# Attention scores whose relative-position biases open the accumulation, one step ahead of the scores (fp32 transformer layer, one core)

## The chip, the cores and the metric

The kernel runs on one NeuronCore of a Trainium2 chip. The metric is the device time of one execution in microseconds (us), the median of several runs.

## The reference

The layer takes `x` of shape (2, 1024, 128) in fp32. It normalises each row, runs attention with 16 heads of 8 dimensions, adds the residual, normalises again, runs expert 0 of a small FFN (128 to 512 to 128, ReLU), normalises with gamma and beta, and adds the residual. The part that matters here is the attention:

```python
q, k, v = (x @ W.T + b, split in 16 heads of 8)
sim  = einsum('bhid,bhjd->bhij', q, k)
sim += transpose(rel_emb[bucket(i - j)], (2, 0, 1)) * SCALE   # 32 buckets; constant from a distance of under 128 on
sim += where(j > i, -inf, 0)
out  = softmax(sim) @ v ; out @ Wo.T + bo
```

The bucket of the far distances gives one constant a head, which cancels in the softmax. So only the "near" strip has a bias that must be added: from the diagonal (where the mask is) to a distance below 128.

## The kernel before, in words

Q and K are split into three bf16 parts each and stored to DRAM, so that a score is one bf16 matmul over 96 rows, plus 2 rows that carry minus the row maximum (`MROW`). The attention works on 8 groups of 4 heads (`G` = 8; 4 groups for each of 2 batches). `QA`, `KA` and the bias table `TT` are double buffered by group (index `p`).

A group has 12 steps, `STEPS`: for the query columns 0 to 511 (`ic` = 0) the key blocks `jb` 0 to 3, then for the columns 512 to 1023 (`ic` = 1) the key blocks 0 to 7. A step is 128 keys by `w` query columns, w = 512, 384, 256, 128 in steps 0 to 3, 512 in steps 4 to 8, then 384, 256, 128 in steps 9 to 11. For step s TensorE makes the scores of 4 heads in PSUM (`ST`, halves q = 0 and 1 of two heads, one bank a head), ScalarE takes the exp of one half at a time (`exps`, two activations a step) into `PT`, and TensorE multiplies by the values (`values`, into `OV`).

There is one set of score banks. So the scores of step s+1, half q, wait until the exp of step s, half q, has read the bank (semaphore `s_exp`). `exps` waits for `s_str`, which counts finished halves of scores.

Steps 0 to 3 and 7 to 11 have a near strip. There the bias is added in PSUM: for each head four matmuls of 32 output rows (the four column strips of the array, which run beside each other) multiply the constant matrix `flb` with a shifted window of `TT`. In the kernel before they come after both halves of the scores, and the last of them lets the exp begin.

Beside this the kernel finds the row maxima of the next group: 39 units (`UNITS`, 0 to 38), each one or a few score matmuls into one of three PSUM banks (`SM`, `NSM` = 3) and a VectorE maximum over it. A unit's matmul waits until VectorE has finished the unit three before it. `places()` spreads the units over the 12 steps and 3 positions of a step (0: after the scores of half 0; 1: after those of half 1; 2: at the end) in proportion to a cost that it estimates for each position. Units 13 and 38 are the transposes ("m") that turn the maxima into rows; their way is VectorE copy to `mrow`, then a DMA by SyncE (`move_m`) into `QA`, and the scores of step 0 (unit 13) or of step 4 (unit 38) of the group wait for it (`s_md`). Units 37 and 38 of a group lie in the group's own step 0, the others in the group before.

TensorE's order in step s (`group`) is: scores of s+1 half 0, units at 0, scores of s+1 half 1, units at 1, biases of s+1, values of s, units at 2. The last step works on step 0 of the next group. The last group has FFN tasks in place of units.

SyncE's queue is in order (`load`): for each group the mrow DMA of half 1, then the loads of the first half of `QA`/`KA` for the group after next, then, once `s_str` says that all 24 halves of the group's scores are done, the loads of the second half and of `TT` (6 DMAs), and behind them the next group's mrow DMA.

The program has loops: VectorE's and ScalarE's run over pairs of groups, TensorE's over groups 2 to 5.

Of the kernel before, what the change touches and what calls it, by code (L numbers as in the profile page):

```python
# [43 lines left out]
KST = MROW + 2  # L44
IC = 512
# [2 lines left out]
LSC = 2048.0  # L48
MASK16 = -60000.0
BW = 384  # L50
NEARU = 240


STEPS = [(ic, jb) for ic in range(N // IC) for jb in range(4 * (ic + 1))]
NSTEP = len(STEPS)
# [3 lines left out]
def step_cols(ic, jb):  # L59

    off = max(0, jb * 128 - ic * IC)
    return off, IC - off
# [28 lines left out]
assert NU % NSM == 0  # L91


NEAR0, NEAR1 = 176, 240

def near_cols(ic, jb):

    i0 = ic * IC + step_cols(ic, jb)[0]  # L100
    out = []
    for c, n in enumerate((NEAR0, NEAR1)):
        end = min(jb * 128 + n, (ic + 1) * IC)
        if end > i0:
            out.append((c, i0 - jb * 128 + 64 - 64 * c, end - i0))
    return out


def unit_cost(u):

    if u[0] == "m":
        return 200
    if u[0] == "far":
        return len(u[2]) * u[4] + 60
    return len(u[2]) * ((128 if u[1] == 0 else 256) + 75)


def places():

    pts, t = [], 0.0
    for s in range(NSTEP):
        ic, jb = STEPS[(s + 1) % NSTEP]
        half = 2 * step_cols(ic, jb)[1] + (640 if near_cols(ic, jb) else 0)
        for pos, cost in enumerate((half, half, 4.2 * step_cols(*STEPS[s])[1])):
            t += cost
            pts.append((t, s, pos))
    costs = [unit_cost(u) for u in UNITS]  # L130
    out, own, done = {}, {}, 0.0
    for u in range(NU):
        at = t * (S_START + (S_END - S_START) * done / sum(costs[:-1]))
        if u == NU - 1:
            at = t * M1_AT
        done += costs[u]
        s, pos = next((s, pos) for c, s, pos in pts if c > at % t)
        (own if at >= t else out).setdefault((s, pos), []).append(u)
    return out, own


S_START, S_END, M1_AT = 0.15, 1.03, 1.06
NEXT_UNITS, OWN_UNITS = places()


# [40 lines left out]
def tasks_at(s):  # L186
    if s not in WITHIN_AT:
        return range(0)
    later = [v for k, v in WITHIN_AT.items() if k > s]
    return range(WITHIN_AT[s], min(later) if later else len(WITHIN))  # L190
# [16 lines left out]
def build(nc, x, early, late, vectors, table, out):  # L207
    ctx = ExitStack()
    with ctx:
        def sb(name, shape, dt=F32):  # L210
            return ctx.enter_context(nc.sbuf_tensor(name, shape, dt))

        def sem(name):
            return ctx.enter_context(nc.semaphore(name))
# [6 lines left out]
        QA = sb("QA", [128, 2, 2, HG, IC], BF16)  # L221
        KA = sb("KA", [128, 2, 2, HG, IC], BF16)
        TT = sb("TT", [128, 2, HG, NEARU], FP16)
        NB = sb("NB", [128, 2, HG, 256], BF16)
# [11 lines left out]
        flb = sb("flb", [128, 64 + 128], BF16)  # L236
# [38 lines left out]
        ST = ps[:, 0:4, :].rearrange("p (b h) n -> p b h n", b=2)  # L275
# [34 lines left out]
        s_ldt = [sem(f"s_ldt{p}") for p in range(2)]  # L310
# [8 lines left out]
        s_str = sem("s_str")  # L319
        s_exp = sem("s_exp")  # L320
# [26 lines left out]
        def _(sp):  # L347
# [36 lines left out]
            def load_tt(hg, p):  # L384
                for part in range(2):
                    sp.dma_start(TT[64 * part:64 * part + 64, p, :, :],
                                 bass.AP(f16_d, hg * (HG * 2 * BW) + part * BW, [[1, 64], [2 * BW, HG], [1, NEARU]])
                                 ).then_inc(s_ldt[p], 16)
# [535 lines left out]
        def _(pe):  # L924
# [55 lines left out]
            def unit(g, p, k):  # L980
# [22 lines left out]
                                                KA[0:KS, p, j // IC, h, j % IC:j % IC + n], start=True, stop=True)  # L1003
                last.then_inc(s_smr, 1)

            def scores(g, p, s, q):

                ic, jb = STEPS[s]
                off, w = step_cols(ic, jb)
                near = near_cols(ic, jb)  # L1010
                if q == 0 and jb == 0:
                    pe.wait_ge(s_md[ic], 32 * g + 32)
                pe.wait_ge(s_exp, 2 * NSTEP * g + 2 * s + q + 1)
                for h in range(2 * q, 2 * q + 2):
                    last = nc.tensor.matmul(ST[:, q, h % 2, off:off + w],  # L1015
                                            KA[0:KST, p, jb // 4, h, (jb % 4) * 128:(jb % 4 + 1) * 128],
                                            QA[0:KST, p, ic, h, off:off + w], start=True, stop=not near,
                                            skip_group_check=True)
                if not near:
                    last.then_inc(s_str, 1)  # L1020

            def biases(p, s):

                ic, jb = STEPS[s]
                off, w = step_cols(ic, jb)
                near = near_cols(ic, jb)
                for q in range(2 if near else 0):
                    for h in range(2 * q, 2 * q + 2):
                        for c, u0, n in near:
                            for e in range(2):  # L1030
                                r0 = 64 * c + 32 * e
                                last = nc.tensor.matmul(ST[r0:r0 + 32, q, h % 2, off:off + n], flb[:, 32 * e:32 * e + 32],  # L1032
                                                        TT[:, p, h, u0:u0 + n], start=False, stop=True,
                                                        skip_group_check=True)
                    last.then_inc(s_str, 1)

            def values(g, p, s):
                ic, jb = STEPS[s]
                off, w = step_cols(ic, jb)
                if jb == 0:  # L1040
                    pe.wait_ge(s_ov, 2 * g + ic + 2)
                pe.wait_ge(s_exp, 2 * NSTEP * g + 2 * s + 4)
                for h in range(HG):
                    last = nc.tensor.matmul(OV[32 * h:32 * h + 2 * HD, off:off + w], VG[:, p, jb, h, :],  # L1044
                                            PT[:, s % 3, h, off:off + w], start=(jb == 0),
                                            stop=(jb == 4 * ic + 3), skip_group_check=True)
                last.then_inc(s_pv, 1)
# [48 lines left out]
            def group(g, p, load, last=False, first=False):  # L1096

                def s_units_at(s, pos):
                    for k in (OWN_UNITS0 if first else OWN_UNITS).get((s, pos), []):
                        unit(g, p, k)  # L1100
                    if not last:
                        for k in (NEXT_UNITS0 if first else NEXT_UNITS).get((s, pos), []):
                            if k in HALF_UNITS:
                                pe.wait_ge(s_ldqk[1 - p][HALF_UNITS[k]], 64 * load)
                            unit(g + 1, 1 - p, k)

                for s in range(NSTEP):
                    if s + 1 < NSTEP:
                        at = (g, p, s + 1)
                    else:  # L1110
                        at = None if last else (g + 1, 1 - p, 0)
                        if not last:
                            pe.wait_ge(s_ldt[1 - p], 32 * load)
                    if at:
                        scores(*at, 0)
                    s_units_at(s, 0)
                    if at:
                        scores(*at, 1)
                    s_units_at(s, 1)
                    if at:  # L1120
                        biases(*at[1:])
                    if s == 0:
                        pe.wait_ge(s_vg, g + 1)
                    values(g, p, s)
                    s_units_at(s, 2)
                    if last:
                        for n in tasks_at(s):
                            task(n)
# [23 lines left out]
            nc.tensor.matmul(ps[0:64, 0, 0:64], flb[:, 0:64], flb[:, 0:64], start=True, stop=True).then_inc(s_pv, 3)  # L1152
            pe.wait_ge(s_ldt[0], 32)
            for q in range(2):
                scores(0, 0, 0, q)
                unit(0, 0, OWN0 + q)
            biases(0, 0)
            group(0, 0, 1, first=True)
            group(1, 1, 2)
            with pe.Fori(1, G // 2 - 1) as r:  # L1160
                for p in range(2):
                    group(2 * r + p, p, r + 1 + p)
# [101 lines left out]
```

## Time and profile before

| | us |
|---|---|
| median of 3 runs | 406.53 (405.81 to 408.67) |
| the profiled execution | 405.76 |
| its span on the core | 403.9 |
| TensorE busy | 321.9 (80%) |
| VectorE busy | 288.2 (71%) |
| ScalarE busy | 183.9 (46%) |
| scores of step 4, groups 0 to 7, begin at | 99.15, 137.99, 173.38, 207.60, 242.07, 276.18, 310.23, 343.15 |

The profile is of one execution; the span leaves out some 2 us around it. Busy times overlap between engines. The last line is the beat of the kernel: one group takes some 34 us, and the eight groups take the stretch from 79 us to 365 us of the span. Its first number is of the group whose start still has a slow TensorE clock.

### The profile page before, as it was taken

The numbers are of one execution on the slowest core, as the hardware profiler recorded it, in microseconds if no ns is written. First come the engines' busy times: TensorE is split into PE (matmuls) and PEld (weight loads), VectorE is DVE, ScalarE is ACT, GpSimd is POOL, SyncE is SP. The second block draws the span as 40 slices with busy tenths as digits, with TensorE's granted clock in tenths as the row PEclk, the third lists the DMA queues.
The fourth block names the chain that finished last, engine by engine and source line by source line (L and its number), as shares of the span: only waits on it lengthen the run. The fifth ranks groups of instructions, "written<-read, shape, count | busy, mean of one in ns | idle before, by whom it ended". The sixth has DMA issues, their size and how long they took to land.

```text
span 403.9 us, 9250 instructions
## 1 busy us (share of the span) xinstructions
PE 321.9 (80%) x3197; PEld 152.9 (38%) x3197; DVE 288.2 (71%) x960; ACT 183.9 (46%) x258; POOL 69.6 (17%) x78
## 2 busy tenths in 40 slices
PE   0282438396999799889989979988998998999982
PEld 0131215143234334434433433443444344346752
DVE  3985356358668478588868848867885996773986
ACT  1042024132555455565555456556455555774330
POOL 9812035700001000100100010010010000161552
PEclk9996586668699899999999999999999999999997
DMA  8013422410011201201110121222123010200011
GB/s 234 17 52 116 144 88 94 147 64 3 3 45 42 60 2 61 84 4 46 60 42 17 49 87 23 76 78 41 38 71 88 15 18 9 33 2 11 4 54 52
DMA packets 18297, 21.95 MB, mean 54 GB/s; under 512 B 5584, under 2 KB 14960, under 8 KB 18256
## 3 DMA queue, kind: packets, MB, share of 16 engines
q1 hardware_dynamic: 18256, 21.45, 18.2%
q8 instruction: 20, 0.33, 0.3%
q14 instruction: 21, 0.17, 0.1%
HBM read 14.98 MB, written 4.23 MB: 48 GB/s over the span
## 4 chain that ended last, share of the span: by engine, by line
PE 47%; DVE 18%; DMA 14%; issue 8%; ACT 5%; SPq 4%; POOL 1%; DVEq 0%; ACTq 0%; POOLq 0%
PE ps L1015 13%; PE ps L1001 12%; PE ps L1044 12%; DMA QA<-mrow 6%; ACT PT L626 5%; PE ps L1032 5%; DMA qk_scratch<-QS 4%; DVE FM L759 4%; DVE junk L766 3%; DVE XN L701 2%; DMA KA<-qk_scratch 2%; DMA rows<-in_vectors 2%; PE ps L1077 2%; DVE st L836 1%; SPq L394 1%
## 5 line engine op out<-in xcount | busy, mean ns | idle before, releaser
L626 ACT ACTIVATE PT<-ps 128x1024 f32<-128x1024 f32 (+1 forms) x192 | 145.8, 810 | 135.4 <-PE ps L1032 106.7
L759 DVE TENSOR_REDUCE FM<-ps 128x1 f32<-128x512 f32 (+3 forms) x176 | 108.5, 660 | 30.3 <-PE ps L1001 29.6
L1001 PE MATMUL ps<-KA,QA 96*128 96x256 bf16 (+3 forms) x544 | 108.7, 293 | 18.4 <-DMA KA<-qk_scratch 14.5
L1015 PE MATMUL ps<-QA,KA 98*128 98x512 bf16 (+3 forms) x384 | 98.1, 341 | 26.1 <-DMA QA<-mrow 9.8
L766 DVE CUSTOM_DVE_ANT_0 junk<-ps,NB 128x256 bf16<-128x256 f32 (+1 forms) x224 | 79.0, 403 | 32.0 <-PE ps L1001 31.7
L1044 PE MATMUL ps<-PT,VG 128*16 128x512 f32 (+3 forms) x768 | 86.6, 497 | 0.0
L1001 PEld LDWEIGHTS ps<-KA,QA 96*128 96x128 bf16 x544 | 44.2, 101 | 105.3 <-DVE FM L759 31.1
L1015 PEld LDWEIGHTS ps<-QA,KA 98*128 98x128 bf16 x384 | 31.8, 100 | 53.8 <-ACT PT L626 25.2
L497 POOL COPY NB<-NBH 128x1024 bf16 (+1 forms) x7 | 7.3, 1041 | 216.7 <-PE ps L1044 215.8
L1032 PE MATMUL ps<-TT,flb 128*32 128x176 f16 (+4 forms) x1152 | 38.9, 245 | 0.0
L1032 PEld LDWEIGHTS ps<-TT,flb 128*32 128x32 bf16 x1152 | 21.5, 96 | 17.7 <-issue 16.9
L1044 PEld LDWEIGHTS ps<-PT,VG 128*16 128x16 f32 x768 | 21.2, 97 | 9.6 <-issue 8.2
L766 DVE DVE_READ_ACCUMULATOR2_ANT FM<- 128x1 f32 x256 | 21.2, 83 | 1.1 <-issue 1.1
L766 DVE CUSTOM_DVE_ANT_0 junk<-ps,NBH 128x256 bf16<-128x256 f32 (+1 forms) x32 | 11.2, 403 | 10.7 <-PE ps L1001 10.5
L932 PE MATMUL ps<-early_s,XN 128*128 128x128 f32 x16 | 4.1, 425 | 18.1 <-DVE XN L701 18.1
L1077 PE MATMUL ps<-QS,late_s 128*128 128x512 f32 x32 | 15.8, 611 | 0.8 <-ACT QS L653 0.8
L754 DVE COPY mrow<-ps 8x512 bf16<-8x512 bf16 x16 | 6.5, 408 | 12.1 <-PE ps L1001 6.5
L545 POOL TENSOR_SCALAR tmp<-mv 128x4 f32<-128x4 f32 x8 | 2.3, 286 | 69.7 <-DVE mv L839 69.7
L585 ACT ACTIVATE QS<-ps,early_s 128x512 bf16<-128x512 f32 x8 | 5.5, 688 | 17.1 <-PE ps L938 17.1
L701 DVE TENSOR_SCALAR XN<-X,mv,rs 128x128 f32<-128x128 f32 x16 | 11.5, 1284 | 0.1
L938 PE MATMUL ps<-xnT,early_s 128*128 128x512 f32 x16 | 11.0, 800 | 0.0
L932 PEld LDWEIGHTS ps<-early_s,XN 128*128 128x128 f32 x16 | 3.2, 224 | 18.9 <-issue 16.4
(88 smaller groups left out, 255.6 us busy)
## 6 DMA issues: line engine op xcount, KB each, us to landing
QA<-qk_scratch SPq DMA_DIRECT2D x48, 96.0 KB
KA<-qk_scratch SPq DMA_DIRECT2D x16, 288.0 KB
TT<-f_scratch SPq DMA_DIRECT2D x16, 120.0 KB, 7.0
qk_scratch<-QS SPq DMA_DIRECT2D x4, 384.0 KB
qk_scratch<-QS SPq DMA_DIRECT2D x12, 128.0 KB
X<-in_x SPq DMA_DIRECT2D x2, 512.0 KB, 6.2
out<-U SPq DMA_DIRECT2D x4, 256.0 KB, 2.3
xnT<-OT SPq DMA_DIRECT2D x28, 32.0 KB
```

Of the source, the lines that this page charges most:

```text
L497: nc.gpsimd.tensor_copy(NB[:, p, :, :], NBH[:, bass.ds(HG * hg, HG), :]).then_inc(s_nb, 1)
L626: nc.scalar.activation(PT[:, s % 3, 2 * q:2 * q + 2, off:off + w], ST[:, q, :, off:off + w], ACT.Exp).then_inc(s_exp, 1)
L701: last = nc.vector.tensor_scalar(XN[:, t, :], X[:, t, :], mv[:, t, 0:1], rs[:, t:t + 1], ALU.subtract, ALU.mult)
L759: nc.vector.tensor_reduce(FM[:, ib, heads[0]:heads[-1] + 1, piece], bank[:, 0:w * len(heads)].rearrange("p (h n) -> p h n", n=w), AX.X, AL ...
L766: last = nc.vector.tensor_tensor_reduce(junk[:, k % NSM, i, 0:w], bank[:, i * w:(i + 1) * w], nb[:, h, 256 - w:256], 1.0, NEG, ALU.add, AL ...
L932: last = nc.tensor.transpose(ps[:, BANK["T", b, half], i * 128:(i + 1) * 128], XN[:, b * TPB + 4 * half + i, :], idf[:, :])
L938: nc.tensor.matmul(ps[:, BANK["QK"[qk], b, c], :], (wq_s, wk_s)[qk][:, :], xnT[:, b, c * IC:(c + 1) * IC], start=True, stop=True).then_inc ...
L1001: last = nc.tensor.matmul(bank[:, i * w + j - j0:i * w + j - j0 + n], QA[0:KS, p, ib // 4, h, (ib % 4) * 128:(ib % 4 + 1) * 128], KA[0:KS, ...
L1015: last = nc.tensor.matmul(ST[:, q, h % 2, off:off + w], KA[0:KST, p, jb // 4, h, (jb % 4) * 128:(jb % 4 + 1) * 128], QA[0:KST, p, ic, h, o ...
L1032: last = nc.tensor.matmul(ST[r0:r0 + 32, q, h % 2, off:off + n], flb[:, 32 * e:32 * e + 32], TT[:, p, h, u0:u0 + n], start=False, stop=Tru ...
L1044: last = nc.tensor.matmul(OV[32 * h:32 * h + 2 * HD, off:off + w], VG[:, p, jb, h, :], PT[:, s % 3, h, off:off + w], start=(jb == 0), stop ...
L1077: last = nc.tensor.matmul(bank, w1_s[:, f * 128:(f + 1) * 128], tT[:, c % 2, :], start=True, stop=True)
```

## The change

Three things change. The bias matmuls of a step are now the first of the accumulation (`start=True`, 240 columns in all four strips, where two strips had 176; 128 columns where the step has no more, 112 in step 7), and they are issued a step ahead: at the end of step s, behind the values, come the biases of step s+2, whose half q waits for the exp of step s+1, half q. The scores of a near step are two matmuls a head: one adds onto the biased columns, one begins fresh on the columns behind them (272 columns in steps 0 and 8, 144 in 1 and 9, 16 in 2 and 10, 400 in 7; none in 3 and 11). Each half of the scores now lets its exp begin by itself. `places()` counts other costs (no bias in the first two positions, 1200 or 450 more in the third), so that units move: unit 3 from the end of step 2 to position 0 of step 3, unit 7 to the end of step 4, unit 14 from step 6 to the end of step 5, others between. `TT` has 304 columns instead of 240, so its DMA rows are 608 bytes instead of 480. The wait for `TT` of the next group stands a step earlier.

```diff
-NEARU = 240
+NEARU = 304
...
-NEAR0, NEAR1 = 176, 240
+NEAR = 240
...
     i0 = ic * IC + step_cols(ic, jb)[0]
-    out = []
-    for c, n in enumerate((NEAR0, NEAR1)):
-        end = min(jb * 128 + n, (ic + 1) * IC)
-        if end > i0:
-            out.append((c, i0 - jb * 128 + 64 - 64 * c, end - i0))
-    return out
+    return max(0, min(jb * 128 + NEAR, (ic + 1) * IC) - i0)
...
-        half = 2 * step_cols(ic, jb)[1] + (640 if near_cols(ic, jb) else 0)
-        for pos, cost in enumerate((half, half, 4.2 * step_cols(*STEPS[s])[1])):
+        half = 2 * step_cols(ic, jb)[1]
+        ahead = 1200 if near_cols(*STEPS[(s + 2) % NSTEP]) else 450
+        for pos, cost in enumerate((half, half, 4.2 * step_cols(*STEPS[s])[1] + ahead)):
...
+            def biases(g, p, s, q):
...
+                pe.wait_ge(s_exp, 2 * NSTEP * g + 2 * s + q + 1)
+                for h in range(2 * q, 2 * q + 2):
+                    for e in range(4):
+                        c, r0 = e // 2, 32 * (e % 2)
+                        nc.tensor.matmul(ST[32 * e:32 * e + 32, q, h % 2, off:off + near], flb[:, r0:r0 + 32],
+                                         TT[:, p, h, u0 - 64 * c:u0 - 64 * c + near], start=True, stop=False,
+                                         skip_group_check=True)
...
-                pe.wait_ge(s_exp, 2 * NSTEP * g + 2 * s + q + 1)
+                if not near:
+                    pe.wait_ge(s_exp, 2 * NSTEP * g + 2 * s + q + 1)
                 for h in range(2 * q, 2 * q + 2):
-                    last = nc.tensor.matmul(ST[:, q, h % 2, off:off + w],
...
-                if not near:
-                    last.then_inc(s_str, 1)
...
+                    for a, b, fresh in ((off, off + near, False), (off + near, off + w, True)):
+                        if b > a:
+                            last = nc.tensor.matmul(ST[:, q, h % 2, a:b],
+                                                    KA[0:KST, p, jb // 4, h, (jb % 4) * 128:(jb % 4 + 1) * 128],
+                                                    QA[0:KST, p, ic, h, a:b], start=fresh, stop=True,
+                                                    skip_group_check=True)
+                last.then_inc(s_str, 1)
...
                 for s in range(NSTEP):
...
                     s_units_at(s, 1)
-                    if at:
-                        biases(*at[1:])
                     if s == 0:
                         pe.wait_ge(s_vg, g + 1)
                     values(g, p, s)
+                    if ahead:
+                        if s + 2 == NSTEP:
+                            pe.wait_ge(s_ldt[1 - p], 32 * load)
+                        for q in range(2):
+                            biases(*ahead, q)
                     s_units_at(s, 2)
```

## Rows read from the trace of the kernel before

**Rows 1.** The page: engines' busy time and instructions, then the costliest groups of instructions.

```profile
PE 321.9 (80%) x3197; PEld 152.9 (38%) x3197; DVE 288.2 (71%) x960; ACT 183.9 (46%) x258; POOL 69.6 (17%) x78
...
L626 ACT ACTIVATE PT<-ps 128x1024 f32<-128x1024 f32 (+1 forms) x192 | 145.8, 810 | 135.4 <-PE ps L1032 106.7
...
L759 DVE TENSOR_REDUCE FM<-ps 128x1 f32<-128x512 f32 (+3 forms) x176 | 108.5, 660 | 30.3 <-PE ps L1001 29.6
...
L1015 PEld LDWEIGHTS ps<-QA,KA 98*128 98x128 bf16 x384 | 31.8, 100 | 53.8 <-ACT PT L626 25.2
...
L1032 PE MATMUL ps<-TT,flb 128*32 128x176 f16 (+4 forms) x1152 | 38.9, 245 | 0.0
```

**Rows 2.** Busy time by engine: steps 6 to 10, 3 to 5, 11 to 3.

```profile
215.70:229.90 14.20, 14.20 (x175) 6.36 (x174) 12.60 (x40) 7.01 (x10) 0.00 (x0) 1.00 0.13 45
207.60:215.70 8.10, 7.72 (x55) 2.73 (x55) 5.85 (x24) 6.20 (x7) 0.00 (x0) 1.00 0.00 0
229.90:242.00 12.10, 9.36 (x137) 4.72 (x135) 7.03 (x33) 5.79 (x10) 1.39 (x2) 1.00 0.23 73
```

**Rows 3.** Timeline of TensorE: start, length, instructions, idle time before them, releaser.

```profile
207.60 0.60 PE L1015 MATMUL ps<-QA,KA 98*128 98x512 bf16 x2 [1.60 <-DMA QA<-mrow]
...
212.28 0.60 PE L1015 MATMUL ps<-QA,KA 98*128 98x512 bf16 x2
...
215.71 0.61 PE L1015 MATMUL ps<-QA,KA 98*128 98x512 bf16 x2
...
216.98 0.39 PE L1001 MATMUL ps<-KA,QA 96*128 96x128 bf16 x4
...
220.68 0.49 PE L1032 MATMUL ps<-TT,flb 128*32 128x176 f16 x14
...
221.11 1.03 PE L1044 MATMUL ps<-PT,VG 128*16 128x512 f32 x6
...
228.18 0.28 PE L1015 MATMUL ps<-QA,KA 98*128 98x128 bf16 x2
...
229.94 0.60 PE L1015 MATMUL ps<-QA,KA 98*128 98x512 bf16 x2
...
233.15 0.50 PE L1015 MATMUL ps<-QA,KA 98*128 98x384 bf16 x2 [0.79 <-ACT PT L626]
...
242.07 0.60 PE L1015 MATMUL ps<-QA,KA 98*128 98x512 bf16 x2 [1.40 <-DMA QA<-mrow]
```

**Rows 4.** Timeline of the SyncE queue: DMA issues.

```profile
195.51 2.60 SPq L379 DMA_DIRECT2D QA<-qk_scratch  x3
...
202.43 15.35 SPq L394 DMA_DIRECT2D QA<-mrow  x4
...
229.59 2.54 SPq L379 DMA_DIRECT2D QA<-qk_scratch  x3
```

**Rows 5.** Timeline of ScalarE, same stretch.

```profile
212.92 1.94 ACT L626 ACTIVATE PT<-ps 128x1024 f32<-128x1024 f32 x2 [0.34 <-PE ps L1015]
...
227.29 1.09 ACT L626 ACTIVATE PT<-ps 128x512 f32<-128x512 f32 x2 [1.44 <-PE ps L1032]
```

**Rows 6.** Timeline of VectorE, same stretch.

```profile
208.57 0.42 DVE L766 CUSTOM_DVE_ANT_0 junk<-ps,NB 128x256 bf16<-128x256 f32 x1 [1.28 <-PE ps L1001]
...
214.71 1.49 DVE L759 TENSOR_REDUCE FM<-ps 128x1 f32<-128x384 f32 x3
...
234.83 0.20 DVE L777 TENSOR_REDUCE NM<-FM 128x16 f32<-128x48 f32 x1
```

**Rows 7.** Chain of waits in order of time (start, length, what).

```profile
232.07 1.03 ACT PT L626
...
235.42 3.10 issue
...
238.71 0.42 DVE mrow L754
...
239.90 2.06 DMA QA<-mrow
```

More of the change, by code:

```diff
@@ L1004, in unit @@
                 last.then_inc(s_smr, 1)
+            def biases(g, p, s, q):
+                ic, jb = STEPS[s]
+                off, w = step_cols(ic, jb)
+                near = near_cols(ic, jb)
+                if not near:
+                    return
+                u0 = ic * IC + off - jb * 128 + 64
+                pe.wait_ge(s_exp, 2 * NSTEP * g + 2 * s + q + 1)
[5 more added lines that the diff above has]
+                                         skip_group_check=True)
             def scores(g, p, s, q):
@@ L1012, in scores @@
                     pe.wait_ge(s_md[ic], 32 * g + 32)
-                pe.wait_ge(s_exp, 2 * NSTEP * g + 2 * s + q + 1)
+                if not near:
+                    pe.wait_ge(s_exp, 2 * NSTEP * g + 2 * s + q + 1)
                 for h in range(2 * q, 2 * q + 2):
-                    last = nc.tensor.matmul(ST[:, q, h % 2, off:off + w],
-                                            KA[0:KST, p, jb // 4, h, (jb % 4) * 128:(jb % 4 + 1) * 128],
-                                            QA[0:KST, p, ic, h, off:off + w], start=True, stop=not near,
-                                            skip_group_check=True)
-                if not near:
-                    last.then_inc(s_str, 1)
[L1022 to L1035, printed above, removed]
+                    for a, b, fresh in ((off, off + near, False), (off + near, off + w, True)):
[5 more added lines that the diff above has]
+                last.then_inc(s_str, 1)
             def values(g, p, s):
@@ L1107, in group @@
                 for s in range(NSTEP):
[L1108 to L1113, printed above, removed]
+                    at, ahead = ((g, p, s + k) if s + k < NSTEP else
+                                 None if last else (g + 1, 1 - p, s + k - NSTEP) for k in (1, 2))
                     if at:
@@ L1154, in _ @@
             for q in range(2):
+                biases(0, 0, 0, q)
+            for q in range(2):
                 scores(0, 0, 0, q)
                 unit(0, 0, OWN0 + q)
-            biases(0, 0)
+            for q in range(2):
+                biases(0, 0, 1, q)
             group(0, 0, 1, first=True)
```

## Prediction

> **What bounds the kernel now.** I read the page first [rows 1]. TensorE is busy 80% of the span. ScalarE waited 106.7 us on the bias matmuls (L1032), which the change is aimed at; but ScalarE is busy only 46%, and its idle time costs something only where another engine then waits for it. So the second view is the busy time by stretch of one group [rows 2]. Steps 6 to 10 are TensorE alone: 14.20 us busy of 14.20, with VectorE at 12.60. In steps 3 to 5 TensorE has 0.38 us of idle time. The idle time is in the change of groups (9.36 busy of 12.10).
>
> The third view is the timeline of TensorE [rows 3], which gives the gaps: 0.79 us at 233.15, where scores wait for an exp, and 1.40 us at 242.07 (1.60 us at 207.60), where the scores of step 4 wait for the mrow DMA.
>
> The fourth view, the SyncE queue [rows 4], says what sets that last wait. The loads at the end of a group's scores start at 195.51, and the scores of step 4 begin at 207.60, 12.1 us later; in the next group 229.59 and 242.07, 12.5 us. The same distance in the four other groups that load is 12.2 to 12.4 us. The mrow DMA is behind these loads in the queue. Issued at 202.43 it ends its wait only some 5 us later, while one issued when they have drained takes 2.06 us [rows 7]. So in most groups the beat is: scores of step 4, then some 22 us to the last `s_str` of the group (207.60 to 229.59), then 12.3 us of loads. What happens in steps 11 and 0 to 3 is hidden behind the loads.
>
> There is a second way to the same point: unit 37, the maxima (234.83 [rows 6]), unit 38, the copy to mrow, the DMA. From the maxima to step 4 this takes 242.07 - 234.83 = 7.2 us where VectorE's loop turns back; 3.10 us of that are "issue" time before the copy [rows 7]. Without them it is some 4.1 us. So this way ends last only in the two groups with a turn of the loop (2 and 4); in the others it would allow step 4 some 2 us earlier than the loads do.
>
> **The bias work itself.** It stays as large. The four strips of a head run beside each other: 16 matmuls occupy 220.68 to 221.11, 0.43 us for four heads, which is 4 x 240 columns at the full clock (granted 1.00 in rows 2, 2.4 GHz). So the two strips that grow from 176 to 240 columns cost nothing; their cover is the two that already had 240. One set leaves the path between scores and exp and stands again behind the values, 0.
>
> **The split scores.** 28 more matmuls a group (7 steps x 4 heads), 224 in all, each with its own weight load (equal counts in rows 1). Columns are the same. Four matmuls of 128 columns with four weight loads take 216.98 to 217.30, with the turn to the bias matmuls in it, so at most 80 ns each and, taking 0.1 us off for that turn, 55 ns: a load is hidden from 128 columns on. The pieces of 16 columns stand alone: 7 ns of columns against a load of some 54 ns, 47 ns each, 4 in step 9 of each group (0.19 us) and 4 in step 1, behind the loads. Lower bound for all pieces: 0.05 us a group; a gain is excluded, as work is only added. Upper bound: each load costs its 100 ns [rows 1], 2.8 us a group. I take 0.2 us between step 3 and the last `s_str`, as in the row of 128 columns the loads are hidden. The Trainium skill ("TensorE: Matmul & The Clock Gate", part 3, The mechanism) says that a weight load overlaps matmuls in flight only when the row group differs. By that rule all 224 loads would show, and the sum would be the upper bound; the row of 55 ns speaks against it, since these loads have the same row group.
>
> **The new wait.** The biases of step s+2, half 1, wait for the exp of step s+1, half 1, and behind them on TensorE are queued the units of position 2, all of the next step, and thereby ScalarE and VectorE. Count from t, the start of the scores of s+1. Exp begins at t + 0.64 (212.28 to 212.92 [rows 3, 5]) and both halves take 1.94, so with 0.05 for the semaphore the wait is over at t + 2.63 at 512 columns. TensorE arrives at 0.43 + units + 0.43 + units + 0.1 (turn) + values 0.86 (the 1.03 at 221.11 less the 0.17 by which a matmul's end trails its columns) + 0.1 + first bias half 0.1 to 0.2. That is 2.41 in step 5 (units 0.38), so 0.22 us of new stall; 2.56 in steps 6 and 7 (units 0.43), 0.07 each; step 8 none (the exps are shorter, 1.51). In step 9 scores of 0.22 twice and values of 0.65 arrive at 1.38 against 0.42 + 1.09 + 0.05 = 1.55, 0.17. Step 10 and step 0 none. Step 11: arrival 1.92 against 2.63, 0.71 us. The last takes the place of the 0.79 us before 233.15 (and of 0.2 us at the half after it): the exps begin 1.5 us earlier there, but now TensorE waits for both halves where it waited for one, before unit 36, the next scores and unit 37.
>
> **The units.** They are the hidden part. Before, unit 3 was done while step 4 waited for the DMA (VectorE idles 1.28 us up to 208.57 [rows 6]); now it is issued after that wait, one reduce (mean 0.66 us [rows 1]) more for VectorE in the part that counts. Before step 5's scores at 212.28 there is one unit more on TensorE, 0.22 us. In step 5 the end position has units 11, 12, 13 and 14. Unit 13 needs the reduce of unit 10, unit 14 that of unit 11. The three reduces of 384 columns begin at 214.71 now and take 0.5 us each; with VectorE 0.6 us later, the second ends near 216.35. Unit 14 stands now ahead of step 6's scores, which began at 215.71, and would hold them to 216.56: 0.85 us later, of which 0.2 is unit 7, 0.22 the new stall, the rest unit 14. To steps 6 to 10 come 0.07 + 0.07 + 0.17 + 0.2 (split), less small changes of order: step 11 begins 231.1 instead of 229.94, +1.1 to 1.2.
>
> **The sum by groups.** The last `s_str` comes earlier in step 10 than it did: it waits neither for biases nor for two units, 0.4 us after the step's start instead of some 1.2. Step 10 starts 1.1 later (228.18 to 229.3), so the loads start at 229.85 instead of 229.59: +0.3 in groups 1, 3, 5 and 6, 4 x 0.3 = 1.2 us, and the rest of the delay is hidden by the loads. Cover gone, it would be 1.1 each. In groups 2 and 4 the maxima come at 235.95 instead of 234.83, 2 x 1.1 = 2.2 us. Group 0 (slow clock, units elsewhere, first biases ahead of the first scores) +0.3. The last group has TensorE full of FFN tasks and no units: the exps start earlier, the new waits and the tasks take it back, -1 to +0.5; with the reciprocals that load VectorE in group 6, I take +0.3. Sum 4.0 us. Against the profiled execution, 405.76 becomes 409.8; the median of 406.53 lies 0.77 higher, so 410.5.
>
> The DMA of `TT` grows from 120 to 152 KB a half. The Trainium skill ("DMA: Bandwidth & Descriptors", its table of limits) puts 512 bytes as the least transfer at full rate, with read-modify-write below. The rows go from 480 to 608 bytes, so by that rule the load would get cheaper instead of dearer. No row here separates its price from the 12.3 us, so the sum has 0, and the range takes 0.3 us a group either way.
>
> **Rivals.** (1) Faster: ScalarE's head start is what counts. The waits of 0.79 and 0.20 us at the change of groups vanish, no unit holds the scores of step 6, and the distance of 12.3 us is the chain of the maxima and not the loads: 7 changes of groups x 0.99 = 6.9, 399.6. For it speaks the large idle time of ScalarE; against it that 12.1 to 12.5 us recurs in six groups with different DMA waits, and the 0.71 that I count in step 11. It decides once TensorE reaches the bias half after the exp has ended.
> (2) No difference: the loads pin the beat and VectorE is not late at unit 14. Then the new stalls of steps 5 to 9 (0.5) are about paid by the shorter way to `s_str` (0.8): 0 to +1.5 us, 406.5 to 408. Against it is VectorE's 12.60 of 14.20.
> (3) Slower by more: the loads do not hide the change of groups, because mrow then ends last everywhere: 7 x 1.1 = 7.7, 414.2. It decides when the delay of the maxima passes 2 us in the unlooped groups.
> (4) The weight loads show: 16 of the 28 a group lie between step 3 and the last `s_str`, 8 x 16 x 0.1 = 12.8 us, 419.3 alone.
> (5) The change does not do what it says: the bias waits so long that exps begin no earlier. Then idle time before the exps stays above 100 us; it ends like (3).
>
> **Chances.** Forecast 0.38 (408.5 to 412.5), (1) 0.13, (2) 0.28, (3) with (5) 0.14, (4) 0.07. The predicted time is the forecast's, 410.5. The range reaches down over (2) and the near part of (1), up over (3): 403 to 416; outside lie some 0.1 below and 0.1 above. 1% (402.5 to 410.6) is about what a measurement of this kernel tells from no change: faster 0.12; the same 0.45, which is (2) and nearly half of the forecast; slower 0.43.
>
> **What would show it.** Bias matmuls with idle time before them, released by ScalarE, mostly in step 11 (0.7) and step 5 (0.2). The 12.3 us from the first load of a run to step 4 kept in groups 1, 3, 5 and 6. Step 6 of a group some 8.9 us after its step 4's scores instead of 8.1. ScalarE's idle time well under 135 us. Weight loads of the 128-column kind 608 instead of 384, with a mean near 100 ns, and TensorE's busy time in steps 6 to 10 grown by under 0.5 us. Wrong would be the prediction if the 12.3 us shrink (then faster), or if the pieces stretch steps 7 to 10 by more than a microsecond.

## The result and the profile after

The changed kernel takes 427.12 us (424.66 to 428.44, 4 runs) against 407.6 of the kernel before beside it (405.81 to 410.97, 4 runs): 1.046 times as long, 95% interval 1.038 to 1.055. The ratios, here and below, leave out executions that took over 1.5% longer than the fastest of their kernel; the medians leave out none. I had predicted 410.5 and 403 to 416. It is slower, as forecast, but by 19 us and not by 4.

The page of the profiled execution (428.44 us, span 426.6), the lines that answer to [rows 1], and one more:

```profile
PE 339.5 (80%) x3421; PEld 172.2 (40%) x3421; DVE 288.3 (68%) x960; ACT 184.5 (43%) x258; POOL 69.4 (16%) x78
...
q8 instruction: 30, 0.49, 0.5%
...
L622 ACT ACTIVATE PT<-ps 128x1024 f32<-128x1024 f32 (+1 forms) x192 | 146.4, 809 | 154.1 <-PE ps L1030 153.9
...
L755 DVE TENSOR_REDUCE FM<-ps 128x1 f32<-128x512 f32 (+3 forms) x176 | 109.0, 660 | 45.8 <-PE ps L997 45.1
...
L1030 PEld LDWEIGHTS ps<-QA,KA 98*128 98x128 bf16 x608 | 52.1, 101 | 47.4 <-issue 17.9
...
L1014 PE MATMUL ps<-TT,flb 128*32 128x240 f16 (+2 forms) x1152 | 47.6, 258 | 7.7 <-ACT PT L622 5.4
```

The 224 extra matmuls and loads are there, with the same 101 ns a load. ScalarE waits more than before (154 us against 135), not less: nothing became faster. The line q8 is the queue that brings TensorE's instructions, in packets of 16 KB (over all the runs below its count changes only with TensorE's program). The page of the kernel before has 20 of them:

```profile
q8 instruction: 20, 0.33, 0.3%
```

The exps do begin sooner behind their own scores. In step 9, at full clock, it is 0.61 us (270.88 to 271.49) where the kernel before has 1.83 us (222.51 to 224.34):

```profile
270.88 0.49 PE L1030 MATMUL ps<-QA,KA 98*128 98x240 bf16 x4
271.49 1.51 ACT L622 ACTIVATE PT<-ps 128x768 f32<-128x768 f32 x2 [1.43 <-PE ps L1030]
```
```profile
222.51 0.49 PE L1015 MATMUL ps<-QA,KA 98*128 98x384 bf16 x2
224.34 1.51 ACT L626 ACTIVATE PT<-ps 128x768 f32<-128x768 f32 x2 [1.21 <-PE ps L1032]
```

But the scores themselves come later by as much: counted from the scores of step 4 (254.75 and 207.60), this exp begins after 16.74 us in both kernels. TensorE is the full engine here, and moving work within it moved the exps nowhere.

Where the time went is told by the starts of step 4's scores, the beat of the kernel. They were 137.99, 173.38, 207.60, 242.07, 276.18 and 310.23 for groups 1 to 6, and are 138.10, 173.73, 210.18, 254.75, 290.26 and 327.10. Group 4's start alone falls back by 10 us. The timeline of TensorE there and in what follows, to be held against [rows 3]:

```profile
238.11 0.39 PE L1014 MATMUL ps<-TT,flb 128*32 128x240 f16 x8 [0.53 <-ACT PT L622]
238.43 0.39 PE L997 MATMUL ps<-KA,QA 96*128 96x256 bf16 x2
243.05 0.48 PE L1030 MATMUL ps<-QA,KA 98*128 98x240 bf16 x2 [4.23 <-issue]
246.34 0.48 PE L1030 MATMUL ps<-QA,KA 98*128 98x240 bf16 x2 [2.80 <-issue]
...
254.75 0.60 PE L1030 MATMUL ps<-QA,KA 98*128 98x512 bf16 x2 [0.88 <-DMA QA<-mrow]
...
263.72 0.60 PE L1030 MATMUL ps<-QA,KA 98*128 98x112 bf16 x4
...
290.26 0.83 PE L1030 MATMUL ps<-QA,KA 98*128 98x512 bf16 x2 [1.88 <-DMA QA<-mrow]
...
291.30 1.06 PE L1030 MATMUL ps<-QA,KA 98*128 98x512 bf16 x2
```

Three things are to be seen. At 238.82, where TensorE's loop over groups turns from group 3 to 4, it stands still for 4.23 us and, two matmuls later, for 2.80 us, and waits for nothing that the profile shows ("issue"). The granted clock falls during the first stop, so the price of the turn is more than the two gaps; the stretch behind it (the column after the engines is the granted clock, 0.50 is 1.2 GHz):

```profile
242.80:249.40 6.60, 3.54 (x18) 1.55 (x22) 1.33 (x7) 1.62 (x2) 0.00 (x0) 0.50 0.09 31
```

Behind 290.26 a pair of score matmuls takes 1.06 us where it takes 0.60 elsewhere: the clock. And the SyncE queue of that group, beside [rows 4], has a longer way from the first load to step 4: 290.26 - 277.16 = 13.1 us, before 12.3.

```profile
277.16 2.28 SPq L375 DMA_DIRECT2D QA<-qk_scratch  x3
...
285.38 1.37 SPq L390 DMA_DIRECT2D QA<-mrow  x2
```

The busy time of 10 us from step 4 on, in group 5 and in group 4:

```profile
290.20:300.20 10.00, 9.70 (x75) 3.95 (x75) 6.49 (x25) 6.40 (x7) 0.00 (x0) 0.83 0.11 16
255.00:265.00 10.00, 9.60 (x92) 4.30 (x90) 8.12 (x30) 6.76 (x8) 0.00 (x0) 1.00 0.17 25
```

TensorE gets 75 matmuls done where it gets 92 done at full clock. A mean of 0.83 is some 3.4 us at the lower level of 1.2 GHz. It falls after the wait for the mrow DMA, here 1.88 us. The same happens after 173.73 and 210.18, and for twice as long after 327.10, but not after 138.10, where the wait was 1.89 us. From group 1 on, the profiled execution of the kernel before has it only in group 1, after its one wait of 2.38 us.

### The profile page after: what moved, and what is told of

Its sections match the earlier page's. It is cut to its first block, busy times and chain, and to the rows that moved or that the text cites. A ratio compares the mean times of both kernels' runs of the same rounds, so it can differ in the third digit from the quotient of the medians.

```text
span 426.6 us, 9700 instructions
## 1 busy us (share of the span) xinstructions
PE 339.5 (80%) x3421; PEld 172.2 (40%) x3421; DVE 288.3 (68%) x960; ACT 184.5 (43%) x258; POOL 69.4 (16%) x78
## 3 DMA queue, kind: packets, MB, share of 16 engines
HBM read 15.51 MB, written 4.23 MB: 46 GB/s over the span
## 4 chain that ended last, share of the span: by engine, by line
PE 48%; DMA 15%; DVE 14%; issue 10%; ACT 8%; SPq 4%; POOL 1%; ACTq 0%; DVEq 0%; POOLq 0%
PE ps L997 13%; PE ps L1030 13%; PE ps L1043 11%; ACT PT L622 8%; DMA QA<-mrow 7%; PE ps L1014 6%; DMA qk_scratch<-QS 4%; DVE FM L755 3%; DVE XN L697 2%; DMA KA<-qk_scratch 2%; DMA rows<-in_vectors 2%; PE ps L1076 1%; DVE st L832 1%; DVE junk L762 1%; DVE U L885 1%
## 5 line engine op out<-in xcount | busy, mean ns | idle before, releaser
L1030 PE MATMUL ps<-QA,KA 98*128 98x240 bf16 (+3 forms) x608 | 98.9, 283 | 24.6 <-DMA QA<-mrow 16.6
L1043 PE MATMUL ps<-PT,VG 128*16 128x512 f32 (+3 forms) x768 | 85.1, 517 | 0.0
L1030 PEld LDWEIGHTS ps<-QA,KA 98*128 98x128 bf16 x608 | 52.1, 101 | 47.4 <-issue 17.9
L1014 PE MATMUL ps<-TT,flb 128*32 128x240 f16 (+2 forms) x1152 | 47.6, 258 | 7.7 <-ACT PT L622 5.4
L1014 PEld LDWEIGHTS ps<-TT,flb 128*32 128x32 bf16 x1152 | 24.6, 97 | 58.0 <-ACT PT L622 42.4
L1043 PEld LDWEIGHTS ps<-PT,VG 128*16 128x16 f32 x768 | 12.7, 96 | 23.0 <-issue 17.0
L841 DVE TENSOR_TENSOR QS<-ps,X 128x512 f32<-128x512 f32 x4 | 2.7, 683 | 12.4 <-PE ps L1067 12.4
```

What stands on the lines that cost most here:

```text
L1014: nc.tensor.matmul(ST[32 * e:32 * e + 32, q, h % 2, off:off + near], flb[:, r0:r0 + 32], TT[:, p, h, u0 - 64 * c:u0 - 64 * c + near], star ...
L1030: last = nc.tensor.matmul(ST[:, q, h % 2, a:b], KA[0:KST, p, jb // 4, h, (jb % 4) * 128:(jb % 4 + 1) * 128], QA[0:KST, p, ic, h, a:b], sta ...
```

## The experiments

The runs of the kernel before spread more than I had thought (405 to 421 us), and the longer ones have the lower clock: the mean granted clock is 0.925 in the one of 405.93 us and 0.890 in the one of 421.03 us. In its profiled execution the waits of 1.4 to 1.6 us before step 4 bring no fall to half clock; b_unroll below, the same kernel but for a loop written out, has four falls in its own. So ratios are given, each against runs of the kernel before beside it on the same chip; of the kernel called b_tt, whose executions spread most, only the range.

**The turn of the loop.** Written out instead of looped, in the changed kernel and in the kernel before:

```diff
-            with pe.Fori(1, G // 2 - 1) as r:
+            for r in range(1, G // 2 - 1):
```

> The changed kernel with TensorE's loop over groups 2 to 5 written out, so that it has no turn; nothing else differs. Theory (instruction fetch: the loop body has outgrown the instruction buffer, and the 4.23 and 2.80 us of idle time behind the turn are its refetch): both gaps vanish, with them the half clock behind them; 8 to 10 us faster than the changed kernel, 417 to 419, some 2.5% above the kernel before. Rival (the gaps are waits of the new order, which merely fall there): they stay, 425 to 428.

Measured (a_unroll): 420.14 us, ratio 1.029 (1.021 to 1.037). Both gaps are gone; the scores behind the bias matmuls of the group change follow at once. That is 7.0 us of the 19.5, a little less than the 8 to 10 expected.

> The kernel before with the same loop written out. Theory: its loop body fits, the turn costs nothing that shows (scores at 233.15 start 0.05 us after the exp that they wait for), so no difference within 1%. Rival (straight code is better or worse for every version, by another way): the same step of 8 to 10 us would appear here, or a loss by more instruction fetching.

Measured (b_unroll): 409.47 us, ratio 0.997 (0.991 to 1.003). In the kernel before the turn costs nothing that can be told from zero. So the loop as such is not the cause. (The profiled execution, 414.15 us, has falls to half clock after its waits of 2.09, 1.75, 1.62 and 1.63 us before step 4: the spread again.) Is it the new order, or the length of the body? The kernel before with split scores, in its old order:

```diff
-                    last = nc.tensor.matmul(ST[:, q, h % 2, off:off + w],
...
+                    cut = off + max([n for _, _, n in near], default=0)
+                    for a, b in ((off, cut), (cut, off + w)):
+                        if b > a:
+                            last = nc.tensor.matmul(ST[:, q, h % 2, a:b],
```

> The kernel before with the scores of near steps in two matmuls a head, in the old order, the biases behind them, units as before: 224 more matmuls and weight loads, and a loop body as long as the changed kernel's. Theory (size of the loop body): a gap of some 7 us behind the turn of TensorE's loop at about 232 us, as in the changed kernel, plus under 0.3 us a group for the pieces: 414 to 417. Rival A (the gap comes from the new order, not from size): no gap, 407 to 409. Rival B (weight loads show, 0.1 us each): 16 to 28 x 0.1 us a group, steps 7 to 10 stretched, 418 or more, with or without the gap.

The output of this kernel leaves the near scores out; it serves for its times alone. Measured (b_split): 416.78 us, ratio 1.020 (1.012 to 1.028). The gaps are there, in the old order, and the instruction queue has its 30 packets:

```profile
239.87 0.50 PE L1018 MATMUL ps<-QA,KA 98*128 98x240 bf16 x4 [3.00 <-issue]
...
243.37 0.59 PE L1035 MATMUL ps<-TT,flb 128*32 128x240 f16 x8 [2.13 <-issue]
```
```profile
q8 instruction: 30, 0.49, 0.5%
```

And the other way round, the new order with a short body:

```diff
-                    for a, b, fresh in ((off, off + near, False), (off + near, off + w, True)):
+                    for a, b, fresh in ((off, off + w, True),):
...
-                                         ST[:, q, :, off:off + w], ACT.Exp).then_inc(s_exp, 1)
+                                         ST[:, q, :, off:off + w], ACT.Exp, scale=1e-3).then_inc(s_exp, 1)
```

> The changed kernel with one fresh matmul a head for the scores (the bias underneath is overwritten, so the output leaves the biases and the mask out; the exp is taken of a thousandth of the score, to keep it finite). TensorE's loop body loses 56 matmuls and 56 weight loads. Theory (size): the gaps behind the turn vanish as in the written-out version, 416 to 419. Rival A (order): gaps stay, 424 to 427. Rival B (weight loads): both the gaps stay and steps 7 to 10 get 0.4 us shorter each.

Measured (a_one): 419.21 us, ratio 1.025 (1.017 to 1.033), no gaps, 20 instruction packets. So the length of the loop body decides, not the order. Of the body, the extra pieces are 28 matmuls and 28 weight loads a group, two groups long. With the short body the queue brings its 20 packets and none comes during the loop's second round (none between 227.5 and 305.4 us in the kernel before, none between 231.4 and 315.2 in a_one); with the long one there are 10 more, 8 of them between 240.2 and 304.4 in the change. And the stops end with them: in the change a packet starts at 240.26 and one at 243.55, and TensorE goes on 2.79 us behind each; in b_split it is 2.58 and 2.51 us (packets at 237.29 and 240.86). Written out, the changed kernel has 27 packets and no stop, so fetching straight on is hidden, and what shows is the fetch after the jump back. That the body no longer fits into what the sequencer keeps is the reading that fits all four runs; the buffer itself no trace shows.

**The width of TT.** The wider table alone, in the kernel before:

```diff
-NEARU = 240
+NEARU = 304
```

> The kernel before with TT 304 columns wide (DMA rows of 608 bytes), nothing else. Theory (the load ahead of the mrow DMA got longer with the wider table): the distance from the first load to the scores of step 4 goes from 12.0 to 12.5 us to 12.6 to 13.2, which is 0.7 x 5 = 3 to 4 us, and the waits before step 4 pass 1.9 us and bring the half clock more often: 411 to 416. Rival (the distance grew because of the new order): unchanged distances and time, within 1%.

Measured (b_tt): 414.78 to 426.68 us in four runs (median 422.78, above the 411 to 416 expected), with the kernel before at 405.95 to 416.38 beside it. The profiled execution is the longest of the four. From the first load to step 4 it is now 12.6 to 13.3 us in all six groups. SyncE's queue, TensorE's step 4 and the 10 us behind one of them:

```profile
202.94 2.60 SPq L379 DMA_DIRECT2D QA<-qk_scratch  x3
...
209.87 1.39 SPq L394 DMA_DIRECT2D QA<-mrow  x2
```
```profile
215.54 1.03 PE L1015 MATMUL ps<-QA,KA 98*128 98x512 bf16 x2 [2.10 <-DMA QA<-mrow]
```
```profile
178.00:188.00 10.00, 10.00 (x50) 3.34 (x51) 5.45 (x23) 6.44 (x7) 0.00 (x0) 0.66 0.00 0
```

The mrow DMA is issued 6.9 us after the first load, as before, but lands later, TensorE waits 1.7 to 3.3 us instead of mostly 1.2 to 1.6, and in this execution each of the six waits is followed by some 6.8 us at 1.2 GHz (0.66 of the clock over 10 us, 50 matmuls for 88). From the scores of step 4 to the last `s_str` it is then 24.5 to 25.0 us, for 21.8 to 22.1 at full clock. In the changed kernel the wide load can be taken back, since columns 240 and on hold zeros:

```diff
+            nc.gpsimd.memset(TT[:, :, :, LOADU:NEARU], 0.0).then_inc(s_zero, 1)
...
-                                 bass.AP(f16_d, hg * (HG * 2 * BW) + part * BW, [[1, 64], [2 * BW, HG], [1, NEARU]])
+                                 bass.AP(f16_d, hg * (HG * 2 * BW) + part * BW, [[1, 64], [2 * BW, HG], [1, LOADU]])
```

> The changed kernel, loops and placement as in the change, but only 240 columns of TT are loaded (rows of 480 bytes, as before); columns 240 to 303 hold no bias and are set to zero once. Theory (three causes: turn of the loop 7 us, wider TT with the half clock behind it, placement of units): the distance from load to step 4 goes back from 12.4 to 13.2 to 12.0 to 12.5 us, 3 to 8 us faster than the changed kernel, 418 to 424, the gaps at the turn stay. Rival (the wide load matters only in the old order): 425 to 428.

Measured (a_zero): 420.52 us, ratio 1.032 (1.023 to 1.042): 6.6 us less than the change. The distances are 12.0 to 12.3 us again (13.3 in group 2, where VectorE's loop turns, and 20.2 in group 4, where both loops turn). The gaps at the turn of TensorE's loop stay, 3.86 and 2.76 us, and end 2.58 and 2.71 us behind a packet of its instruction queue.

**The placement of the units.** The changed kernel, loop written out, with the old costs in `places()`:

```diff
-        half = 2 * step_cols(ic, jb)[1]
-        ahead = 1200 if near_cols(*STEPS[(s + 2) % NSTEP]) else 450
-        for pos, cost in enumerate((half, half, 4.2 * step_cols(*STEPS[s])[1] + ahead)):
+        half = 2 * step_cols(ic, jb)[1] + (640 if near_cols(ic, jb) else 0)
+        for pos, cost in enumerate((half, half, 4.2 * step_cols(*STEPS[s])[1])):
```

> The changed kernel, loop written out, and units placed by the old costs. Theory (unit 14 ahead of step 6's scores and unit 3 behind step 4's wait make each group 0.5 to 0.9 us longer from step 4 to the last s_str): 22.4 goes to 21.8, 2 to 4 us faster than the written-out version, 415 to 418. Rival (placement doesn't matter, the waits for exps do): 419 to 421.

Measured (a_unroll_units): 415.35 us, ratio 1.012 (1.006 to 1.018), 4.8 us less than with the new placement. The timeline of group 2:

```profile
170.73 0.61 PE L1029 MATMUL ps<-QA,KA 98*128 98x512 bf16 x2 [1.29 <-DMA QA<-mrow]
...
179.00 0.61 PE L1029 MATMUL ps<-QA,KA 98*128 98x112 bf16 x4
```

The scores with which TensorE opens its step 6 (they are those of step 7, hence the pieces of 112 columns) begin 8.27 us after the scores of step 4, with unit 14 behind them; in the change it is 263.72 - 254.75 = 8.97. From the scores of step 4 to the last `s_str` it is 21.6 to 21.9 us in groups at full clock, where the change has 22.4 to 22.6 and the kernel before 21.8 to 22.1.

**What pins the beat.** If the loads ahead of mrow do, it should help to put the two TT loads of a group behind the next mrow DMA:

```diff
                 move_m(p, 1, g)
+                if g:
+                    load_tt((g + 1) % GPB, 1 - p)
...
                 load_half(g + 2, p, 1)
-                load_tt(hg, p)
...
-            with sp.Fori(0, G // 2 - 2) as r:
+            for r in range(G // 2 - 2):
```

> The kernel before with the two TT loads of a group issued behind the next mrow DMA instead of before it, and SyncE's loop written out for that. Theory (the beat is 12.3 us of loads ahead of the mrow DMA, and TT is part of them): the mrow DMA is issued at the same time but lands 1 to 3 us earlier in five groups; the wait before step 4 falls under 1 us and the half clock behind it vanishes: 398 to 403. Rival (the other loads, of QA and KA, are the backlog, or the wait has another source): 405 to 408.

Measured (b_late): 397.7 us (396.41 to 399.78), ratio 0.971 (0.962 to 0.980), a faster kernel than both. SyncE's queue and TensorE's step 4 in group 3:

```profile
191.96 2.12 SPq L379 DMA_DIRECT2D QA<-qk_scratch  x3
...
199.17 1.28 SPq L394 DMA_DIRECT2D QA<-mrow  x2
200.49 1.37 SPq L386 DMA_DIRECT2D TT<-f_scratch  x2
```
```profile
203.22 0.60 PE L1017 MATMUL ps<-QA,KA 98*128 98x512 bf16 x2 [0.43 <-DMA QA<-mrow]
```

The mrow DMA, issued 7.2 us after the first load (6.9 before), now has its scores running 4.05 us later instead of 5.2 (202.43 to 207.60 in [rows 4] and [rows 3]). The wait is 0.43 us instead of 1.60, and no stretch at 1.2 GHz follows any step 4, not even behind the wait of 2.37 us in group 2. The distance from the first load to step 4 is 10.7 to 11.3 us in four of the six groups, where it was 12.1 to 12.4; in groups 2 and 4, where VectorE's loop turns, it is 13.35 and 11.9. SyncE's loop is written out here too, but the way gets shorter in groups 1, 3, 5 and 6 alike and not only at its turn. The same in the changed kernel, loop written out:

> The changed kernel, TensorE's loop written out, with the two TT loads behind the next mrow DMA. Theory (wider loads ahead of mrow, and the half clock that follows the long wait, make up most of what is left): distances 12.6 to 13.2 fall under 12, no half clock behind step 4: 403 to 410, 10 us or more faster than the written-out version. Rival (the rest is the new order's own): above 415.

Measured (a_late): 408.74 us, ratio 1.001 (0.996 to 1.005): 11.4 us faster than the written-out version. Its longest wait is now in group 2, 3.39 us, where VectorE's loop turns ahead of the copy to mrow; a fall to half clock of 3.4 us follows it, the only one behind a step 4 from group 1 on.

**What the new order is worth by itself.** All side effects out: loop written out, 240 loaded columns, old placement, TT behind mrow.

> The change with its three side effects taken out: TensorE's loop written out, 240 loaded columns, units by the old costs, and the TT loads behind the mrow DMA. What is left is the new order and the split scores. Theory (new order costs 0.5 us of waits for exps a group and gives nothing): 398 to 402, 1 to 4 us behind the same version of the kernel before (397.7). Rival (once the rest is gone, exps that start earlier win): 390 to 396.

Measured (a_best): 402.48 us, ratio 0.988 (0.983 to 0.994), just above the 398 to 402 expected. With one score matmul a head on top (as in a_one):

> As the one above, but one fresh score matmul a head (leaves out biases and mask, exp of a thousandth of the score). Theory (a hidden weight load a piece, 47 ns only for the pieces of 16 columns): 1 to 2 us faster than it. Rival (weight loads show, 28 x 0.1 us a group): over 10 us faster.

Measured (a_best_one): 400.62 us, ratio 0.985 (0.979 to 0.991). That is 1.9 us less, but not all of it is the price of the 224 pieces. In groups at full clock the two kernels are alike: 21.54 to 21.55 us from the scores of step 4 to the last `s_str` in both, and 32.27 and 32.23 us from step 4 to step 4 (groups 5 to 6). So the pieces cost under 0.1 us a group, and the rest of the 1.9 us goes with the longer falls to half clock at the turns of VectorE's loop (10.2 and 3.4 us in the profiled execution of a_best, 6.8 us in this one). The kernel before with the same DMA order is at 397.7, so some 5 us were still open. They might be the order, or the turn of VectorE's loop, which comes in two groups:

```diff
-            with dve.Fori(0, G // 2 - 1) as r:
+            for r in range(G // 2 - 1):
```

> The kernel before with TT loaded behind the mrow DMA, and VectorE's loop over pairs of groups written out too. Theory (with the loads gone from the way of mrow, its turn of 3.1 us before the copy to mrow ends last in groups 2 and 4, where step 4 still waited 2.37 and 1.00 us): 393 to 396. Rival (fetching straight code costs as much): 397 to 400.

Measured (b_late_dve): 392.9 us, ratio 0.964 (0.958 to 0.970). The two turns cost 4.8 us once the loads were out of the way (by the ratios 0.7%, some 3 us, but the times of the two kernels do not overlap: b_late took at least 396.41 us, this one at most 393.8). Then the decisive pair, both without any turn of VectorE's loop:

> The change with its side effects taken out (TensorE's loop written out, 240 loaded columns, units by the old costs, TT behind the mrow DMA) and VectorE's loop written out as well. It differs from the run beside it in the new order and the split scores alone. Theory A (the 5 us by which the new order trailed came from the turns of VectorE's loop, whose 3.1 us land on a longer way and bring the half clock; elsewhere a group takes 32.3 us in both): 391 to 394, within 1% of the other. Theory B (the waits for exps and the pieces cost 0.6 us a group everywhere): 396 to 399.

> The kernel before with TT behind the mrow DMA and VectorE's loop written out, again, for a comparison on one chip. Both theories: 391 to 394.

Measured: 392.92 us (a_best_dve), ratio 0.961 (0.955 to 0.967), and 392.72 us (b_best), ratio 0.959 (0.953 to 0.966). No difference. So the same two turns of VectorE's loop cost the new order 9.6 us (402.48 to 392.92), twice what they cost the old one: as long as that loop stays, the new order is 4.8 us behind (402.48 against 397.7), and falls to half clock follow its waits at these turns, where b_late has none. The SyncE queue of the new order, first loads of groups 3 and 4:

```profile
185.53 2.12 SPq L375 DMA_DIRECT2D QA<-qk_scratch  x3
...
217.58 2.12 SPq L375 DMA_DIRECT2D QA<-qk_scratch  x3
```

and its busy time between them, then that of the old order over its group:

```profile
185.50:217.60 32.10, 31.29 (x394) 16.04 (x392) 25.84 (x95) 19.06 (x27) 1.38 (x2) 1.00 0.13 46
```
```profile
191.10:223.40 32.30, 30.90 (x368) 13.83 (x364) 25.89 (x95) 18.96 (x27) 1.38 (x2) 1.00 0.14 46
```

A group takes 32.05 us in the one and 32.3 in the other, at full clock in both. The new order has no gap at the change of groups (the old one keeps its 0.79 us before the scores of step 1), and TensorE is busy 0.4 us longer a group. That the gained gap pays for the waits for exps and the pieces is my reading; the runs show the sum.

## Why the prediction was wrong

The direction was that of the forecast (though I gave "the same within 1%" 0.45 and "slower" only 0.43), and much of the mechanism held; the size was out by a factor of almost five. Two terms that I had at nothing, the turn of TensorE's loop and the wider TT, are 13.6 of the 16.6 us by which the measured 427.1 lies above my 410.5. The differences, each from two kernels that differ in one thing:

| | counted | measured |
|---|---|---|
| turn of TensorE's loop | not named | 7.0 us (427.1 to 420.1) |
| wider TT | 0, bound 0.3 us a group | 6.6 us (427.1 to 420.5) |
| placement of the units | most of the 4 us | 4.8 us (420.1 to 415.4) |
| new order and pieces, VectorE's loop written out | waits 0.5, pieces 0.2 us a group | none in sum (392.9 and 392.7) |
| the same, VectorE's loop kept | the same | 4.8 us (402.5 and 397.7) |

Not all of them ran on one chip. By the ratios to the kernel before beside them, the first three are 7.2, 5.6 and 6.9 us and the last is 7.1 us, so each is good to some two microseconds; and each carries its share of falls to half clock, so they need not add up.

**The loop: the step that failed.** Under "The split scores" I priced 28 matmuls a group by their columns and weight loads and found them hidden. That was right where I looked: under 0.1 us a group at full clock, against the 0.2 counted. But instructions also have to be brought to the engine: at the turn TensorE stood still for 4.23 and 2.80 us, and its clock was at half for 6.8 us from 242.7 on. The kernel before turned its loop without a gap, so no row of it showed this price, and I took the price of a longer body for zero without saying so. b_split shows it in the old order, a_one shows the new order without it.

**TT: a term wrongly at zero.** I wrote that no row separates its price from the 12.3 us, and put 0. Yet I had just argued that everything ahead of the mrow DMA in the queue is in the beat. By my own argument 64 KB more per group had to count. It is some 0.7 us a group (12.6 to 13.3 us in b_tt), and the rest comes behind it: with the wait before step 4 near 2 us the clock falls in most groups, which adds 1.3 us (23.7 for 22.4, once to half clock for 3.4 us) to 2.8 us (24.8 for 22.0, in b_tt) to the group. The Trainium skill ("DMA: Bandwidth & Descriptors", Specifications) gives 512 bytes as the least transfer at full rate; by that the load should have become cheaper, as its rows grew from 480 to 608 bytes. Here it brings 27% more bytes too, and the way behind it is longer, so any gain from the row length is smaller than what the bytes cost; the runs decide.

**The clock.** I read granted 1.00 in the rows of one execution and took it as given. The same rows show the waits of 1.40 and 1.60 us, and in the same trace the one of 2.38 us in group 1 was followed by a fall. That was the warning. The clock also goes with the spread of the kernel before, from 405 to 421 us.

**The beat: right for the kernel before, too short for the change.** That loads of 12.3 us pin step 4 was confirmed by b_late, which takes TT out of them and gains 10 us or more. But the 12.3 us that I said would be kept in groups 1, 3, 5 and 6 became 12.8, 12.4, 13.1 and 13.2. With b_late rival (3) and the reverse of it, rival (1), fall: the distance was not the chain of the maxima. Rival (1) also expected ScalarE's head start to pay. I too had named idle time of ScalarE well under 135 us as a sign of being right; it is 154 us. That is also the sign of rival (5), above 100 us, but exps do begin sooner behind their scores (0.61 us for 1.83), so its reason, that the bias waits hold them up, falls. Rival (2) needed VectorE not to be late at unit 14, and it is late. Rival (4), weight loads that show, falls by a_best_one (at most 1.9 us for 224 pieces; 0.1 us each would be 22). I had set the rule of the Trainium skill ("TensorE: Matmul & The Clock Gate", part 3, The mechanism) on row groups aside for the row of 55 ns, and the run agrees.

**The waits for exps and the units: right in size.** The scores that open TensorE's step 6 were foretold 8.9 us after the scores of step 4 and come 8.97 us after; unit 14 is issued at 263.54, directly before them. From the scores of step 4 to the last `s_str` at full clock, 22.25 us follow from the prediction's numbers, and it is 22.4 to 22.6. In step 11 the second bias half waits: the first eight bias matmuls run at 237.19, the others at 238.11, 0.7 us of lost time as counted. What I did not expect is that these waits cost nothing in the end in the pair without side effects and without turns of VectorE's loop.

## What to carry to other kernels

A change that adds a few per cent of instructions to a looped engine has a price that no row of the kernel before shows: look at the instruction queue's packets and for "issue" gaps at the turn of the loop, and try the loop written out. Two such side effects can feed each other: the turns of VectorE's loop cost the new order 9.6 us and the old one 4.8. When a DMA with a short message (here a row of maxima) sets the beat, all that is ahead of it in its queue is in the beat too, and widening any of it can cost more than the 0.7 us a group of its bytes, while reordering it is nearly free: 0.971 of the time here, and 0.964 with VectorE's loop written out. A wait of some 2 us on TensorE often costs the wait and then a stretch at half clock behind it.

## What the runs showed of the hardware that was not expected

- With some 364 matmuls and as many weight loads a group (a loop body of two groups), TensorE's loop turned without a gap; with 392 a group it stood still for 4.23 and 2.80 us (3.00 and 2.13, 3.86 and 2.76 in two other kernels), and its instruction queue moved 30 packets of 16 KB instead of 20. Each of these six stops ended 2.5 to 2.8 us after such a packet had started.
- The length of TensorE's wait before step 4 does not decide by itself whether the granted clock falls to 0.5. Falls came at waits of 1.14 us (a_best, group 4), 1.45 us (b_split, group 2) and most of those from 1.5 us on; none came at 1.60 us (before, group 3), 1.89 us (the change, group 1), 2.37 us (b_late, group 2) and 2.40 us (a_one, group 5). A fall lasts some 3.4, 6.8 or 10.2 us.
- VectorE's loop turn takes 3.1 us of issue time; it shows only when it ends last, and then cost 4.8 us for two turns in the old order (397.7 to 392.9) and 9.6 us in the new one (402.5 to 392.9).
